# A graph network on one core: the attention loop reads its targets' parts with 16 products of 24 columns, and its round begins with the scan

## The reference, cut to what matters

```
def gat_layer(x, src, dst, W, a_src, a_dst, b):
    h = (x @ W).reshape(N, H, C)                       # N 12500, H 8, C 8
    alpha_s = jnp.einsum('nhc,hc->nh', h, a_src)
    alpha_d = jnp.einsum('nhc,hc->nh', h, a_dst)
    e = jax.nn.leaky_relu(alpha_s[src] + alpha_d[dst], NEG_SLOPE)
    m = jax.ops.segment_max(e, dst, num_segments=N)
    ex = jnp.exp(e - m[dst])
    denom = jax.ops.segment_sum(ex, dst, num_segments=N)
    alpha = ex / (denom[dst] + 1e-16)
    out = jax.ops.segment_sum(h[src] * alpha[:, :, None], dst, num_segments=N)
    return out.reshape(N, H * C) + b
```

## Time and profile before

| what | value |
|---|---|
| median of 3 runs | 19895.47 us (19890.38 to 19895.66) |
| the profiled execution: its own time | 19894.99 us |
| the profiled execution: its span | 19893.2 us |
| mean granted clock of TensorE over the span | 0.61 |
| PE busy | 14629.5 us (74%) |
| DVE busy | 13457.3 us (68%) |
| POOL busy | 11319.2 us (57%) |
| ACT busy | 5956.9 us (30%) |

### The profile page before, as it was taken

One profiled execution on the slowest core, in us unless ns is written; L12 is line 12 of the kernel. 1 busy time (PEld: TensorE's weight loads), 2 busy tenths in 40 slices (PEclk: granted clock), 3 DMA queues, 4 the chain that ended last, 5 costly groups with the idle time before them and its releaser, 6 DMA issues. The chain is left out here.

```text
span 19893.2 us, 417676 instructions
## 1 busy us (share of the span) xinstructions
PE 14629.5 (74%) x100095; PEld 11369.9 (57%) x100096; DVE 13457.3 (68%) x32082; ACT 5956.9 (30%) x17808; POOL 11319.2 (57%) x11773
## 2 busy tenths in 40 slices
PE   3443337599994999997999979999687777763333
PEld 2322225366663788885888858888556666443332
DVE  4877769477776777777777777777755555543334
ACT  0111129155552333332333323333241111320000
POOL 0477740177772566663666636666307777137775
PEclk7555555577776555555555555555596666875555
DMA  5233334133333222222222222222293222651112
GB/s 185 67 94 94 94 83 123 45 103 103 103 102 66 51 52 51 51 48 47 51 51 51 51 44 51 51 52 51 64 414 66 53 53 53 249 232 26 26 26 46
DMA packets 1474203, 1652.65 MB, mean 83 GB/s; under 512 B 976447, under 2 KB 1080911, under 8 KB 1442001
## 3 DMA queue, kind: packets, MB, share of 16 engines
q1 hardware_dynamic: 1062709, 1057.28, 18.0%
q0 software_dynamic: 404480, 528.97, 13.8%
q10 hardware_dynamic: 6912, 65.18, 0.8%
HBM read 1028.20 MB, written 626.36 MB: 83 GB/s over the span
## 5 line engine op out<-in xcount | busy, mean ns | idle before, releaser
L1724 POOL DMA_INDIRECT gat_from_src<-gat_src_dram,gat_src_at x4992 | 4813.3, 964 | 3227.2 <-issue 1418.1
L2156 POOL DMA_INDIRECT rel_from_src<-typed_dram,rel_src_at x3328 | 3169.5, 952 | 2405.9 <-ACT rel_src_at L2170 1393.4
L1903 PE MATMUL gat_ps_dst<-again_gat_here,gat_memberT 128*128 x29952 | 3011.5, 179 | 69.3 <-DVE gat_memberT L1791 68.1
L1903 PEld LDWEIGHTS gat_ps_dst<-again_gat_here,gat_memberT 128*128 128x128 bf16 x29952 | 2481.2, 103 | 705.1 <-issue 70.1
L2286 PE MATMUL rel_ps_sum<-all_node,rel_msg 128*64 128x128 f32 x6656 | 1517.1, 403 | 1672.2 <-DVEq L2248 1643.1
L1274 POOL DMA_INDIRECT all_node<-hyp_dst_dram,hyp_src_at x1768 | 1717.2, 971 | 1623.5 <-ACT hyp_src_at L1292 1098.9
L1933 PE MATMUL gat_ps_sum<-all_node,gat_msg 128*80 128x128 f32 x9984 | 2484.8, 431 | 47.9 <-DVE gat_msg L1818 5.7
L2286 PEld LDWEIGHTS rel_ps_sum<-all_node,rel_msg 128*64 128x64 f32 x6656 | 1212.7, 210 | 1923.5 <-DVEq L2248 1501.0
L1878 DVE TENSOR_TENSOR gat_sums<-gat_sums,gat_ps_sum 80x128 f32 x4992 | 1393.8, 279 | 1227.8 <-PE gat_ps_sum L1933 746.2
L1933 PEld LDWEIGHTS gat_ps_sum<-all_node,gat_msg 128*80 128x80 f32 x9984 | 2022.6, 251 | 110.1 <-issue 25.6
L776 POOL DMA_INDIRECT bucket_dram<-all_node,order_index x1664 | 1612.8, 969 | 531.5 <-issue 506.6
(11 more groups left out here) (445 smaller groups left out, 26481.8 us busy)
## 6 DMA issues: line engine op xcount, KB each, us to landing
typed_dram<-typed_res SPq DMA_DIRECT2D x200, 2144.0 KB
gat_relrow<-in_rows_dram SPq DMA_DIRECT2D x624, 256.0 KB
all_node<-gcn_table_dram SPq DMA_DIRECT2D x1664, 48.0 KB
gat_from_src<-gat_src_dram,gat_src_at POOLq DMA_INDIRECT x4992
bucket_dram<-by_dst_zero ACTq DMA_DIRECT2D x48, 1326.0 KB
gsum_rec<-bucket_dram SPq DMA_DIRECT2D x221, 288.0 KB
all_node<-lo_rows_dram SPq DMA_DIRECT2D x221, 256.0 KB
rel_table<-inv_count_dram SPq DMA_DIRECT2D x1664, 32.5 KB
```

The source lines that it names most:

```text
L1724: nc.gpsimd.indirect_dma_start(from_src[:, q, k, :], None, g.gat_src[:, :], bass.IndirectOffsetOnAxis(ap=src_at[:, q, k:k + 1], axis=0)).t ...
L1903: last = nc.tensor.matmul(dst_v[:, k, :], memberT[:, q % 2, w, k, :], own[:, w, n, :], start=w + n == 0, stop=w + n == 3)
L2156: nc.gpsimd.indirect_dma_start(from_src[:, q, k, :], None, g.typed[:, :], bass.IndirectOffsetOnAxis(ap=src_at[:, q, k:k + 1], axis=0)).the ...
```

## The change

- `read_dst` multiplies each 0/1 matrix once by all three parts side by side, 24 columns, and adds only over the two blocks: 16 products in place of 48. The three parts land beside each other in PSUM, and a new step on VectorE, `of_targets`, adds them up; `logits` adds the source parts to that.
- The second 0/1 matrix is no longer compared by VectorE. ScalarE makes it in two steps of 1024 columns (`far_distances`, `far_ones`), the last two of its round, behind the exponential of the shift. TensorE and SyncE wait for them.
- The maxima (`top`) have two places. The carry is read straight from the place of the group before, so that `carry_on` is gone; `shift_by` and `shift_down` become one operation.
- VectorE's round begins with the first scan, now one group ahead in place of two; the window registers are loaded between the two scans. `turned_ones` is three groups ahead in place of four.

The lists after: VectorE maxima_so_far 1, windows 0, maxima 1, rescale 0, shift_by 1, turned_ones 3, add 0, of_targets 2, add 1, logits 2, add 2, leaky_logits 2, arguments 1, add 3 to 5, tops_of 1, messages 1, add 6 and 7. ScalarE has far_distances 4 and far_ones 4 behind exp_shift. TensorE's list and SyncE's are the same.

```diff
...
-        step_a, step_b, step_c, opened, cleared, mark_a, mark_p = ph.sems(
-            "step_a step_b step_c opened cleared mark_a mark_p")
+        step_a, step_b, step_c, opened, cleared, mark_a, mark_p, far_off, far = ph.sems(
+            "step_a step_b step_c opened cleared mark_a mark_p far_off far")
         mark_s = ph.sem("mark_s")
...
         memberT, relrow = ph.sb("memberT", [P, 2, 2, K, P], BF16), ph.sb("relrow", [P, 2, CE], BF16)
+        far_d = ph.sb("far_d", [P, CE], BF16)
         leaky = ph.sb("leaky", [P, 2, K, H])
-        carry, top = ph.sb("carry", [H, 2]), ph.sb("top", [H, CE])
+        top = ph.sb("top", [H, 2, CE])
         arg = ph.sb("arg", [P, K, H])
...
         ps_dst, ps_top = ph.ps("ps_dst", [P, 512]), ph.ps("ps_top", [P, 512])
-        dst_v = ps_dst[:, 0:K * H].rearrange("p (k h) -> p k h", k=K)
+        dst_v = ps_dst[:, 0:3 * K * H].rearrange("p (k c) -> p k c", k=K)
         top_v = ps_top[:, 0:K * H].rearrange("p (k h) -> p k h", k=K)
...
                 def load_rows(c, q, i):
...
                     alone(sp, mark_s)
+                    sp.wait_ge(far_off, free2(c))
+                    alone(sp, mark_s)
                     sp.dma_start(relrow[:, q % 2, :], g.in_rows[ds(c * CE, CE)].partition_broadcast(P)).then_inc(rel_in[q], 16)
...
             def _(act):
-                for q in (staged, gather_at, apart, members, expo, shift_e):
+                for q in (staged, gather_at, apart, members, expo, shift_e, far_off, far):
                     act.sem_inc(q, START)
+                act.wait_ge(cleared, 3)
                 def targets(c, q, i):
...
                     nc.scalar.activation(member[:, q], off[:, :, :], ACT.Relu, scale=-1.0, bias=1.0).then_inc(members, 1)
+                def far_distances(c, q, i):
+                    act.wait_ge(rel_in[q], 16 * (i + 1))
+                    act.wait_ge(far, free1(c))
+                    alone(act, mark_a)
+                    nc.scalar.activation(far_d[:, :], relrow[:, q % 2, :], ACT.Abs, scale=-1.0, bias=lane2[:, 0:1]
+                                         ).then_inc(far_off, 1)
+                def far_ones(c, q, i):
+                    act.wait_ge(far_off, ready(c))
+                    act.wait_ge(dst_at, free2(c))
+                    nc.scalar.activation(memberT[:, q % 2, 1].rearrange("p k e -> p (k e)"), far_d[:, :], ACT.Relu,
+                                         scale=-1.0, bias=1.0).then_inc(far, 1)
                 def exponents(c, q, i):
...
                 def exp_shift(c, q, i):
...
                     nc.scalar.activation(shift[:, 1:2], shift[:, 0:1], ACT.Exp).then_inc(shift_e, 1)
-                rounds(act, [(exponents, 1), (targets, 6), (distances, 2), (fields, 4), (zero_ones, 2), (exp_shift, 2)])
+                rounds(act, [(exponents, 1), (targets, 6), (distances, 2), (fields, 4), (zero_ones, 2), (exp_shift, 2),
+                             (far_distances, 4), (far_ones, 4)])
             @block.vector
...
                 v.memset(sums[:, :], 0.0).then_inc(cleared, 1)
-                v.memset(carry[:, :], -BIG).then_inc(cleared, 1)
+                v.memset(top[:, 1, CE - 1:CE], -BIG).then_inc(cleared, 1)
                 v.tensor_scalar(lane2[:, :], g.lane[:, :], float(P), None, ALU.add).then_inc(cleared, 1)
...
                     v.tensor_scalar(memberT[:, s, 0].rearrange("p k e -> p (k e)"), relrow[:, s, :], g.lane[:, 0:1], None,
-                                    ALU.is_equal)
-                    v.tensor_scalar(memberT[:, s, 1].rearrange("p k e -> p (k e)"), relrow[:, s, :], lane2[:, 0:1], None,
                                     ALU.is_equal).then_inc(turned, 1)
                 def tops_of(c, q, i):
...
                     v.tensor_tensor(arg[:, :, :], leaky[:, q % 2], top_v, ALU.subtract).then_inc(back_u, 1)
+                def of_targets(c, q, i):
+                    dve.wait_ge(dst_at, ready(c))
+                    v.tensor_reduce(leaky[:, q % 2], dst_v.rearrange("p k (n h) -> p k h n", n=3), AX.X, ALU.add
+                                    ).then_inc(step_a, 1)
                 def logits(c, q, i):
-                    dve.wait_ge(dst_at, ready(c))
+                    dve.wait_ge(step_a, c * 2 + 1)
                     dve.wait_ge(got[q], 16 * K * (i + 1))
-                    v.tensor_tensor(leaky[:, q % 2], dst_v, from_src[:, q, :, D:D + H], ALU.add).then_inc(step_a, 1)
+                    v.tensor_tensor(leaky[:, q % 2], leaky[:, q % 2], from_src[:, q, :, D:D + H], ALU.add
+                                    ).then_inc(step_a, 1)
                 def leaky_logits(c, q, i):
                     one = leaky[:, q % 2].rearrange("p k h -> p (k h)")
-                    dve.wait_ge(step_a, c + 1)
+                    dve.wait_ge(step_a, c * 2 + 2)
                     v.scalar_tensor_tensor(one, one, LRELU, one, ALU.mult, ALU.max).then_inc(logit, 1)
...
                     dve.wait_ge(mask_in[q], 16 * 2 * (i + 1))
-                    v.tensor_tensor_scan(log_flat, masks[:, q, 0, :], log_flat, carry[:, 1 - s:2 - s], ALU.add,
+                    v.tensor_tensor_scan(log_flat, masks[:, q, 0, :], log_flat, top[:, 1 - q % 2, CE - 1:CE], ALU.add,
                                          ALU.max).then_inc(step_b, 1)
-                def carry_on(c, q, i):
-                    dve.wait_ge(step_b, c * 4 + 1)
-                    v.tensor_copy(carry[:, q % 2:q % 2 + 1], log_flat[:, CE - 1:CE]).then_inc(step_b, 1)
                 def maxima(c, q, i):
-                    dve.wait_ge(step_b, c * 4 + 1)
-                    dve.wait_ge(back, free1(c))
-                    v.tensor_tensor_scan(top[:, ::-1], masks[:, q, 1, ::-1], log_flat[:, ::-1], -BIG, ALU.add, ALU.max
+                    dve.wait_ge(step_b, c * 2 + 1)
+                    dve.wait_ge(back, free2(c))
+                    v.tensor_tensor_scan(top[:, q % 2, ::-1], masks[:, q, 1, ::-1], log_flat[:, ::-1], -BIG, ALU.add, ALU.max
                                          ).then_inc(step_b, 1)
                 def shift_by(c, q, i):
-                    dve.wait_ge(step_b, c * 4 + 3)
-                    v.tensor_tensor(shift[:, 0:1], carry[:, 1 - q % 2:2 - q % 2], top[:, 0:1], ALU.subtract
-                                    ).then_inc(step_b, 1)
-                def shift_down(c, q, i):
-                    dve.wait_ge(step_b, c * 4 + 4)
-                    v.tensor_scalar(shift[:, 0:1], shift[:, 0:1], 0.0, None, ALU.min).then_inc(scanned, 1)
-                own = []
-                def own_window(c, q, i):
-                    own[:] = bases(nc, ENG.DVE, g.base, c, 0, 1)
+                    dve.wait_ge(step_b, c * 2 + 2)
+                    dve.wait_ge(shift_e, free1(c))
+                    v.tensor_scalar(shift[:, 0:1], top[:, 1 - q % 2, CE - 1:CE], top[:, q % 2, 0:1], 0.0, ALU.subtract,
+                                    ALU.min).then_inc(scanned, 1)
                 def rescale(c, q, i):
-                    v.tensor_tensor(sums[:, ds(own[0], 1)], sums[:, ds(own[0], 1)], ps_top[0:rows, K * H:K * H + 1],
+                    dve.wait_ge(back, ready(c))
+                    v.tensor_tensor(sums[:, ds(regs[0], 1)], sums[:, ds(regs[0], 1)], ps_top[0:rows, K * H:K * H + 1],
                                     ALU.mult).then_inc(shifted, 1)
...
                     return step
-                rounds(dve, [(windows, 0), (own_window, 1), (add(0), 0), (add(1), 0), (logits, 2), (add(2), 0),
-                             (leaky_logits, 2), (arguments, 1), (add(3), 0), (add(4), 0), (add(5), 0), (tops_of, 1),
-                             (messages, 1), (maxima_so_far, 2), (carry_on, 2), (maxima, 2), (add(6), 0), (shift_by, 2),
-                             (add(7), 0), (shift_down, 2), (rescale, 1), (turned_ones, 4)])
+                rounds(dve, [(maxima_so_far, 1), (windows, 0), (maxima, 1), (rescale, 0), (shift_by, 1), (turned_ones, 3),
+                             (add(0), 0), (of_targets, 2), (add(1), 0), (logits, 2), (add(2), 0), (leaky_logits, 2), (arguments, 1),
+                             (add(3), 0), (add(4), 0), (add(5), 0), (tops_of, 1), (messages, 1), (add(6), 0),
+                             (add(7), 0)])
             @block.tensor
...
                 def read_dst(c, q, i):
...
                     pe.wait_ge(turned, ready(c))
+                    pe.wait_ge(far, ready(c))
                     pe.wait_ge(logit, free1(c))
...
                         for w in range(2):
-                            for n in range(3):
-                                last = nc.tensor.matmul(dst_v[:, k, :], memberT[:, q % 2, w, k, :], own[:, w, n, :],
-                                                        start=w + n == 0, stop=w + n == 3)
+                            last = nc.tensor.matmul(dst_v[:, k, :], memberT[:, q % 2, w, k, :],
+                                                    own[:, w, :, :].rearrange("p n h -> p (n h)"),
```

(3 more changed lines are left out.)

## The result

The changed kernel took **19440.39 us** (median of four runs, 19427.75 to 19443.19), the kernel before 19892.93 us (four runs beside them on the same chip). The ratio is **0.9772, 95% interval 0.9755 to 0.9789**: 2.3% faster, 452 us. Predicted were 19,490 us, within 19,230 to 19,740. The profiled execution of the changed kernel took 19427.75 us with a span of 19426.0.

A forecast was written before the change was run, and what follows sets the result against it. After the change a closed chain through VectorE and TensorE, its pieces summing to 10.88 us a round against 11.53, was to bound the kernel: 624 x (11.53 - 10.88) = 406 us off 19895, so 19,490 us, range 19,230 to 19,740.

The forecast's parts named there:

- the closed chain: One round from shift through turned maxima, second-half products, sums, messages and two scans back to shift: 10.88 us; chance 0.72.
- TensorE's order: Second-half products stand behind the turned maxima, so VectorE waits about 1.3 us before sum 4 in every round.
- TensorE's load: TensorE's round becomes 9.0 us, busy about 83% of the loops, with 1.8 us idle.
- 16 x 0.132 = 2.1 us: TensorE's 16 weight-load and product pairs a round, each 0.119 us plus 0.013 us for 16 more columns; bounds 1.9 and 3.6.
- The clock: TensorE's granted clock in the attention loops was to go down from 0.58 towards 0.50.
- ScalarE: Two new operations over 128x1024 add 2.1 us a round; exponents end at 2.8 us, messages want them at 4.4 us.
- rival 3: ScalarE's two new operations delay the messages from 1.86 us each; at 2.43 us, 20,220 us; chance 0.07 with unseen waits.
- The reduction: VectorE's new reduction of 128x192 out of PSUM: 0.35 us, some 0.27 us start to start; bounds 0.21 and 0.69 us.
- GpSimd: Eight gathers need 10.21 us, under 10.88; GpSimd still waits for messages some 0.9 us a round with its usual 0.3.
- rival 1: GpSimd's gathers set the round if the chain is under 10.21 us: 19,071 us; chance 0.13 shared with Rival 2 and between.
- Rival 2: VectorE's waits between dependent sums vanish, three intervals becoming 0.28 us each: round 10.36 us, 19,165 us; chance 0.02.
- Rival 4: Some five hand-overs on the chain each cost 0.13 us more: round 11.53 us, no gain, 19,895 us; chance 0.03.

The follow-up runs named there:

- the kernel with TensorE kept busy: The changed kernel plus 56 unread products of 128 bf16 columns a round before the turned maxima: 19130.21 us, 0.9615 of the kernel before.
- the kernel with the products first: The changed kernel with the second half of the products before the turning of the maxima in TensorE's list: 19069.2 us, 0.9584 of the kernel before.
- the old order: The changed kernel with VectorE's list in the order of the kernel before, all else as changed: 19483.86 us, 0.9787 of the kernel before.

## Why the prediction was right, point by point

**The bound moved from TensorE to the closed chain: right**, shown twice. Taking the products out of the chain, and making the same instructions on it shorter, each cut the time by over 300 us, though TensorE already had 4.2 us of idle time a round.

**The chain's pieces.** Measured in the round shown, predicted in brackets: shift to the turned maxima 0.34 us (0.29); to the products 1.18 (1.20); to sum 4 2.13 (2.13); sums 4 and 5 0.62 (0.62); tops 0.13 (0.14); messages 0.60 (0.68); sum 6 to the scan 0.92 (0.94); first scan 2.38 (2.38); second 2.21 (2.20); rescaling 0.10 (0.15). That is 10.61 us. The turn costs 0.72 less 0.23 us once in four rounds, 0.12 a round (0.15). Sum 10.73 us in the timeline, 10.77 by the busy sum, 10.88 predicted. The largest miss, 0.08 us, is the messages: I had read busy time where the next sum starts before it ends. The gain is 467 us between the spans where 406 were said; the 0.11 us of the round, times 624, are 69 us and account for those 61.

**TensorE's order: right**, the wait ahead of sum 4 in every round 1.46 us (1.3 said). **TensorE's load: wrong**, 61% busy where 83% was said, and 4.2 us idle where 1.8 was said. The step that failed is "16 x 0.132 = 2.1 us": the 16 pairs took 0.62 us a round. **The clock went the other way** as well: 0.50 was forecast for the loops and 0.68 was granted, up from 0.58. But the clock is not what made the pairs short. Windows of this line alone (PE busy with its count, PEld busy with its count, the granted clock third from the end): one round of the new kernel at each clock, its loop, and the same 16 pairs in the loop of the kernel with TensorE kept busy:

```profile
10044.99:10045.60 0.61, 0.61 (x16) 0.53 (x15) 0.50 0.16 27
10034.30:10034.80 0.50, 0.50 (x16) 0.43 (x15) 1.00 0.36 55
...
9200.00:11300.00 2100.00, 119.09 (x3072) 125.92 (x3072) 0.68 0.26 54
...
9300.00:11000.00 1700.00, 341.91 (x2656) 254.24 (x2656) 0.92 0.26 58
```

At 0.50 they take 0.61 us in the new kernel, at 0.92 they take 341.91 / 166 = 2.06 us in the other. The prediction took 0.119 us as the price of a pair; it is the mean of a stretch whose pairs come at two rates, as the last section shows, and all 16 of the new kernel come at the quick one. Its remark that this stretch gains from the higher clock is wrong by the same rows. The first half of the products is the part that the clock explains: 1.09 us at 1.00 and 1.98 at 0.50, about 1.4 in the mean of the loop (both halves are 662.3 us in 194.5 rounds, less the 2.00 us of the second; about 2.0 was said). All this cost the forecast nothing, since what ran faster was off the chain, and the products on it still took 2.00 us at 0.50. That is in part luck: the clock rose against the forecast, and with the high clock over the products on the chain the kernel kept busy took 19,130 us, below the stated range. A forecast that had made TensorE's load the bound would have failed with it.

**ScalarE: right.** 1.15 and 1.06 us (1.06 each said), exponents done 2.87 us after the shift (2.8 said), 1.5 us ahead of their need; rival 3 asked for 1.86 us each. **The reduction: right**, 0.35 us busy and 0.27 us start to start, as said. That the second comparison lies wholly in cover when it is on VectorE, as the wait of 1.46 us suggests, was not shown: its experiment ran only on the disturbed chip.

**GpSimd: partly wrong.** It was to wait 0.9 us a round for the messages, its usual 0.3 in it; it waited for them in 26 of 167 rounds. With 10.77 us a round and 10.15 to 10.21 us of its own, the room was 0.6 us. Of it 0.5 us a round are in the list of waits: the 34.5 us, and 49 of the 444.7 us put down to "issue", which is what they exceed 0.3 us a gather by. So rival 1, which needed a chain 0.67 us shorter than forecast, was nearer than it looked: 0.56 us shorter was enough.

**Rival 2 fell.** The waits between VectorE's dependent operations are there: 0.23 us ahead of the scan in the round shown, 59.9 us in 168 rounds with those of the turn, and sums in a pair take 0.70 us (0.28 each alone). The Trainium skill ("VectorE: DVE Perf Modes", The DRAIN you can't avoid) has it, from a row of eight copies, that a semaphore after each operation costs nothing extra; for these small dependent sums the idle time in this trace says otherwise, and the measurement decides. **Rival 4 fell**: the one crossing to TensorE cost 0.05 us more than taken, and the others nothing.

**The scan at the head of the round: no separate gain.** The prediction counted no term for it but its shelter for the register loads. Undone alone, it changed the round by 0.01 us, by two effects of some 0.8 us each that cancel, and neither stands in the prediction.

**Where the gain comes from: partly wrong.** The prediction had also laid the whole gain on fewer products. The kernel with 48 shows that two thirds of it, 297 of 452 us, come without that, from the same 48 pairs in shorter stretches (4.26 us a round, 4.83 before). Which part of the change does this, the comparison moved to ScalarE, the order or the two buffers of maxima, no run takes apart. A forecast for the 48 products by the prediction's rows would have kept TensorE at 11.53 us.

**Slips in the working, without effect on the sum.** TensorE's steps from the shift end at 9.3 us, not 9.1. ScalarE's work is 4.2 us a round by the earlier trace rows, so with 2.1 more 6.3, not 6.7 (measured 1174.28 / 195 = 6.0). By rival 3's own terms the messages wait from 1.88 us on, not 1.86, and its upper bound gives 12.0 us.

## What to carry to other kernels

When the full engine is relieved, write down the closed chain that the new order makes, shift to shift, and then every engine's own total: here they were 10.77, 10.2 (GpSimd) and 6.6 us (TensorE, 61% of 10.77), and only 0.6 us lay between the new bound and the next one. A wait in each direction between two engines, once in each round (VectorE for a product, TensorE for the shift), is a sign to look for a step that stands in an engine's order ahead of something that doesn't need it: here changing the places of two steps in one list gave another 1.9%, nearly as much as the whole change. Look for that swap before cutting more instructions: 32 of 48 products taken away earned 0.8%. And time the stretch to be shortened in many rounds, and its instructions inside it, before dividing it by their number: here it came in two lengths, and its pairs at two rates.

## What the runs showed of the hardware

**The granted clock rose while TensorE got less busy.** Before, it was busy 99% of the loop at a mean granted clock of 0.58; after, 61% busy at 0.68. Within a round, after 4.3 us of idle, the turned maxima and the products ran at 0.50 (1.2 GHz); behind them and the turned logits, all back to back, the clock was at 1.00 (2.4 GHz) for the last eight products, and in the idle stretch that follows it fell (0.65 as its mean). In the kernel with the products first the f32 products come after the pairs and there the clock was 0.50 in both. The busy share doesn't put the kernels in order: that kernel was 78% busy in its loop at 0.59, the one with 48 products 99% at 0.59, the one with the old order 67% at 0.65. With 56 small bf16 products in the idle time it was 1.00 over the chain's products and 0.92 over the loop. What decides between the levels these runs don't tell; that work without a result bought 1.6% is measured.

**Pairs of weight load and product come at two rates, and the clock sets neither.** Windows of this line alone inside single stretches. The kernel before, a long stretch (two windows) and the start of a short one:

```profile
10001.50:10002.00 0.50, 0.50 (x11) 0.48 (x10) 0.50 0.22 32
10003.00:10005.00 2.00, 2.00 (x17) 1.61 (x17) 0.50 0.13 18
10036.40:10037.00 0.60, 0.60 (x22) 0.60 (x21) 0.50 0.30 50
```

The kernel with 48 products, the start of one stretch and the later part of another:

```profile
10006.10:10006.60 0.50, 0.50 (x19) 0.50 (x18) 0.50 0.43 83
...
10019.00:10021.00 2.00, 2.00 (x17) 1.50 (x16) 0.96 0.09 18
```

At the start of a stretch a pair can come every 0.03 us (22 in 0.60 us, 19 in 0.50). Later one comes every 0.12 us: 17 in 2.00 us at 0.50 and at 0.96, and the 16 pairs of the kernel with TensorE kept busy took 2.06 us in the mean at 0.92. So the length of a stretch depends on how many of its pairs come at the quick rate. The long stretch had 11 in its first half microsecond, where the short ones had about 20, and two stretches at 0.50 in the kernel before took 5.42 and 4.20 us. The 16 pairs came at the quick rate where TensorE had idled for 4.3 us a few microseconds before (0.62 us a round), in between (299.92 / 167 = 1.80 us) in the kernel with the products first, with waits of 1.0 and 1.1 us, and at the slow one where it had hardly idled (2.06 us). That looks like a store of prepared work that fills while TensorE has little to do and runs empty in a dense stretch; no run separates this from other causes, and it stays open.

**One chip was a quarter slower.** On one chip the unchanged kernel took 25,370 and 25,084 us, 26 to 28% more, with idle stretches of 1 to 2 us inside groups of TensorE instructions at places without a wait, and 0.70 us for a DMA issue of SyncE's that took 0.28 us elsewhere. Two edits, the swapped order and TensorE kept busy, were slower than before there (1.0136, 1.0395) and faster elsewhere (0.9584, 0.9615). Why, no run shows.
